# Mamba decay matrices in a two-layer kernel: a clamp and one exponential per head on ScalarE, where TensorE added a mask and ScalarE took four exponentials

## The reference

```
dA    = dt * A                                # dt > 0, A < 0: every step is negative
cum   = cumsum(dA)                            # falls along the positions of a chunk
diff  = cum[i] - cum[j]                       # per head
decay = exp(where(i >= j, diff, -inf))        # lower triangle alone, values at most 1
scores = (C_i . B_j) * decay * dt_j
Y_diag = scores @ x ;  states are carried from chunk to chunk
hidden = rmsnorm((Y + D * x) * silu(gate)) * norm_w ;  out = hidden @ out_proj_w
```

## Time and profile before

| what | value |
|---|---|
| median of three runs | 2167.99 us |
| the profiled execution | 2167.26 us, its span 2165.5 us |
| TensorE busy | 2007.6 us, 93% |
| DVE busy | 1610.2 us, 74% |
| ScalarE busy | 1274.9 us, 59% |
| POOL busy | 785.5 us, 36% |
| mean granted TensorE clock | 0.988 |
| DMA | 180.20 MB, mean 83 GB/s |
| the chain that ended last | PE 47%, issue 27%, ACT 11%, DVE 11% |
| ScalarE L1190, the four exponentials per head | 1024 instructions, 288.1 us |
| TensorE L859, the mask | 256 instructions, 77.5 us |

### The profile page before, as it was taken

One profiled execution on the slowest core, in us unless ns is written; L12 is line 12 of the kernel. 1 busy time (PEld: TensorE's weight loads), 2 busy tenths in 40 slices (PEclk: granted clock), 3 DMA queues, 4 the chain that ended last, 5 costly groups with the idle time before them and its releaser, 6 DMA issues.

```text
span 2165.5 us, 43621 instructions
## 1 busy us (share of the span) xinstructions
PE 2007.6 (93%) x12940; PEld 1652.1 (76%) x12940; DVE 1610.2 (74%) x2956; ACT 1274.9 (59%) x3110; POOL 785.5 (36%) x1128
## 2 busy tenths in 40 slices
PE   5999989999899998999989999999999999999997
PEld 4888577777688857777778885777778887677776
DVE  4774589999677458888867745888887773588886
ACT  3562388888555227777745513777774552477775
POOL 2210157777300014556530001556661000155565
PEclk9999999999999999999999999999999999999999
DMA  5330233333322002323322200232232220133321
GB/s 188 116 124 1 83 103 131 131 131 126 112 78 75 32 25 74 94 90 87 92 75 87 77 30 17 88 95 87 87 97 83 83 72 1 40 89 94 94 87 54
DMA packets 100366, 180.20 MB, mean 83 GB/s; under 512 B 8337, under 2 KB 30033, under 8 KB 100177
## 3 DMA queue, kind: packets, MB, share of 16 engines
q1 hardware_dynamic: 100304, 179.40, 26.3%
HBM read 139.52 MB, written 39.85 MB: 83 GB/s over the span
## 4 chain that ended last, share of the span: by engine, by line
PE 47%; issue 27%; ACT 11%; DVE 11%; POOL 2%; ACTq 1%; DVEq 1%; DMA 0%; POOLq 0%
PE bank L650 21%; DVE conv_acc L1337 5%; PE bank L893 4%; ACT conv_acc L1101 4%; PE bank L770 4%; ACT place L1183 4%; PE bank L868 3%; PE bank L876 3%; DVE y_in L1467 3%; PE bank L859 3%; PE bank L750 3%; PE bank L778 2%; ACT bank L1190 1%; PE bank L792 1%; DVE place L1472 1%
## 5 line engine op out<-in xcount | busy, mean ns | idle before, releaser
L650 PE MATMUL bank<-xn_r,w_r 128*128 128x512 f32 x2304 | 587.9, 404 | 18.9 <-issue 9.2
L650 PEld LDWEIGHTS bank<-xn_r,w_r 128*128 128x128 f32 x2304 | 421.9, 191 | 113.8 <-issue 24.7
L1337 DVE SCALAR_TENSOR_TENSOR conv_acc<-bank,conv_sb,conv_acc 128x511 f32<-128x511 f32 (+2 forms) x408 | 304.4, 746 | 97.9 <-ACT conv_acc L1101 80.2
L1190 ACT ACTIVATE bank<-bank,cum_neg 128x128 f32<-128x128 f32 x1024 | 288.1, 361 | 47.3 <-PE bank L859 44.2
L1031 ACT ACTIVATE place_r<-bank 128x512 fp32r<-128x512 f32 (+1 forms) x384 | 199.2, 563 | 177.7 <-PE bank L650 151.5
L1269 DVE TENSOR_TENSOR place_r<-bank,place_r 128x512 fp32r<-128x512 f32 (+1 forms) x384 | 231.0, 641 | 87.7 <-ACT place_r L1031 86.7
L650 PE MATMUL bank<-place_r 128*128 128x512 f32 (+3 forms) x1536 | 284.6, 333 | 5.3 <-DVE place_r L1269 4.5
L650 PEld LDWEIGHTS bank<-place_r 128*128 128x128 f32 x1536 | 236.9, 191 | 23.0 <-DVE place_r L1269 9.5
L543 POOL TENSOR_TENSOR carry<-state,dec 128x128 f32<-128x128 f32 x256 | 105.2, 411 | 407.1 <-ACT state L1026 385.6
L517 POOL TENSOR_TENSOR rstd<-var_eps,minus_half 128x4 f32<-128x4 f32 (+2 forms) x12 | 9.7, 807 | 665.9 <-DVE var_eps L1282 665.9
L1055 ACT ACTIVATE place<-bank,bias 128x512 f32<-128x512 f32 (+3 forms) x256 | 131.4, 526 | 161.0 <-DVE bias L1317 161.0
(11 more groups left out here) (142 smaller groups left out, 3544.6 us busy)
## 6 DMA issues: line engine op xcount, KB each, us to landing
w_r<-pair_split SPq DMA_DIRECT2D x96, 512.0 KB, 4.3
w_r<-qkv_split SPq DMA_DIRECT2D x48, 512.0 KB, 4.0
wo_r<-out_split SPq DMA_DIRECT2D x96, 256.0 KB, 2.6
pair_split<-w_r SPq DMA_DIRECT2D x32, 512.0 KB, 3.3
qkv_split<-w_r SPq DMA_DIRECT2D x16, 768.0 KB, 3.8
w_r<-qkv_split SPq DMA_DIRECT2D x48, 256.0 KB, 3.1
raw<-in_w_pair SPq DMA_DIRECT2D x32, 256.0 KB, 3.5
out_split<-wo_r SPq DMA_DIRECT2D x32, 256.0 KB, 2.0
```

The lines of the kernel that those rows point to most:

```text
L650: ins = mm(out, lhsT=w(a), rhs=m(b), start=(start and i == 0), stop=(stop and i == 2), **kw)
L1190: ins = A(bank[3 + h][:, c * P:(c + 1) * P], bank[3 + h][:, c * P:(c + 1) * P], ACT.Exp, bias=cum_neg[:, c, bass.ds(n * 2 + h, 1)])
L1337: stt(out=conv_acc[:, back:W], in0=src[:, 0:W - back], scalar=conv_sb[:, ch, TAPS - 1 - back:TAPS - back], in1=conv_acc[:, back:W], op0=AL ...
```

## The change

`causal_bf` is no longer added by TensorE: `mask_cum` and its calls go, and with them its wait for `grow`. `mixes` waits for `grow` itself (ScalarE's own `decays`). It then takes Relu(cum_j - bank) per chunk, that is max(cum_j - cum_i, 0), with the positive `cum_t` as bias and a scale of -1, in place in PSUM; it signals a semaphore of its own, waits for it, and takes one exponential exp(-value) over the head's whole bank of 512 columns. On and below the diagonal this is the same decay; above it the clamp gives exp(0) = 1, and the triangle is applied by multiplying `cb` with `upto` when DVE takes it out of PSUM, once per sequence. `causal_bf` and `ident_bf` stay for the attention stage.

```diff
@@ TensorE: mamba_start, and the loop over pairs
-                pe.wait_ge(s_cum_neg_ready, b + 1)
+                pe.wait_ge(s_cum_t_ready, b + 1)
                 pe.wait_ge(s_ffn_hid, b * FT + 7)
                 spread_cum(b, 0, 0)
                 ffn_down(b)
-                mask_cum(b, 0)
...
-            def mask_cum(b, n):
-
-                pe.wait_ge(s_grow_ev, b * NPAIR + n + 1)
-                for h, done in ((0, s_cum0_done), (1, s_cum1_done)):
-                    mm(bank[3 + h][:].rearrange("p (t i) -> p t i", t=NT), lhsT=causal_bf[:],
-                       rhs=ident_bf[:].unsqueeze(1).to_broadcast([P, NT, P]), start=False, stop=True,
-                       skip_group_check=True).then_inc(done, 1)
...
-                    if more:
-                        mask_cum(b, n + 1)
                     make_states(b, n, par)
                     in_block(b, n, par)
@@ ScalarE
                 def mixes(n, par, h):
 
-                    act.wait_ge((s_cum0_done, s_cum1_done)[h], b * NPAIR + n + 1)
+                    act.wait_ge(s_grow_ev, b * NPAIR + n + 1)
                     for c in range(NT):
-                        ins = A(bank[3 + h][:, c * P:(c + 1) * P], bank[3 + h][:, c * P:(c + 1) * P], ACT.Exp,
-                                bias=cum_neg[:, c, bass.ds(n * 2 + h, 1)])
+                        ins = A(bank[3 + h][:, c * P:(c + 1) * P], bank[3 + h][:, c * P:(c + 1) * P], ACT.Relu,
+                                bias=cum_t[:, c, bass.ds(n * 2 + h, 1)], scale=-1.0)
+                    ins.then_inc((s_span0, s_span1)[h], 1)
+                    act.wait_ge((s_span0, s_span1)[h], b * NPAIR + n + 1)
+                    ins = A(bank[3 + h][:], bank[3 + h][:], ACT.Exp, scale=-1.0)
                     ins.then_inc((s_mix_exp0, s_mix_exp1)[h], 1)
@@ DVE, once per sequence
-                dve.tensor_copy(cb[:].rearrange("p t i -> p (t i)"), bank[1][:]).then_inc(s_cb_ev, 1)
+                tt(cb[:], bank[1][:].rearrange("p (t i) -> p t i", t=NT), upto[:].unsqueeze(1).to_broadcast([P, NT, P]),
+                   ALU.mult).then_inc(s_cb_ev, 1)
                 dve.wait_ge(s_cum_turned, b + 1)
-                ts(cum_neg[:], bank[6][:].rearrange("p (t h) -> p t h", t=NT)[:, :, 0:MH], -1.0, None, ALU.mult).then_inc(s_cum_neg_ready, 1)
+                ts(cum_t[:], bank[6][:].rearrange("p (t h) -> p t h", t=NT)[:, :, 0:MH], 1.0, None, ALU.mult).then_inc(s_cum_t_ready, 1)
```

More of the change, by code:

```diff
@@ L157, in two_layers @@
         pick = sb("pick", [P, 2, 2], F32R)
-        cum_neg = sb("cum_neg", [P, NT, MH])
+        cum_t = sb("cum_t", [P, NT, MH])
         state = sb("state", [P, NT - 1, P])
@@ L228, in two_layers @@
         s_gate_ready = sem("gate_ready")
-        s_cum0_done = sem("cum0_done")
-        s_cum1_done = sem("cum1_done")
+        s_span0 = sem("span0")
+        s_span1 = sem("span1")
         s_mix_exp0 = sem("mix_exp0")
@@ L278, in two_layers @@
         s_cum_turned = sem("cum_turned")
-        s_cum_neg_ready = sem("cum_neg_ready")
+        s_cum_t_ready = sem("cum_t_ready")
         s_pick_ready = sem("pick_ready")
```

## The result

| | median us | runs us |
|---|---|---|
| before | 2168.28 | 2166.64 to 2169.62 |
| after | 2260.36 | 2259.48 to 2261.13 |

The ratio is 1.0425, 95% interval 1.0407 to 1.0443: slower by 92 us. Forecast were 2273 us and the range 2240 to 2325.

The account below looks back on a forecast made before the run. ScalarE's fixed-order list was to set the step: 8.31 + 1.26 = 9.57 us against 8.76, 72.9 us over sequences 1 to 3, plus 31.5 in sequence 0; with the end 105 us, giving 2273 us, range 2240 to 2325.

Parts of the forecast that it names:

- The two rings: Pair steps, sequences 1 to 3: the longer of ScalarE's loop (8.31 us, then 9.57) and TensorE with DVE's (8.58) sets the step.
- The mask was nearly free: TensorE's mask matmuls in each pair step: removing them shortens the loop through TensorE by 0.18 us, not 0.60, because DVE's `pair_gate` is next.
- rival B: Pair stage: ScalarE's idle time absorbs the added exponentials, DVE and TensorE set 8.58 us per step, 2146 us; chance 0.04.
- The exponential's price: ScalarE, per head: 512-column exponential 0.60 us plus 0.03 gap at its wait, 0.63 us; 1.26 per pair; bounds 0.52 to 1.02.
- The unmodified part of ScalarE's ring: ScalarE from decays through its first tap and DVE back to decays, without added work: 5.21 + 3.10 = 8.31 us.
- Edits at nothing: DVE's `cb` product, `cum_t` for `cum_neg`, and the sequence start: at most 1 us per sequence, taken as nothing.
- Who else waits: Users of later exponentials: states' copy 0.63 us later, POOL's carry 6.06 us behind decays; TensorE keeps 0.99 us of slack.
- Rival A: Pair stage: TensorE's gaps lower its clock, projections lengthen; if every third pair, 64 us more, 2337 us; chance 0.08.
- C: ScalarE: Relu and Exp in different function tables, two switches per head at 1.28 us, 657 us more, 2825 us; chance 0.01.

Follow-up runs that it names:

- half exponential: The changed kernel with each head's new exponential over 256 of the 512 columns: 2205.73 us, steps of 9.02 us in sequences 1 to 3.
- squares moved: The changed kernel with ScalarE's `squares` of pair n-2 put behind the next pair's `gate_tanh`, into the wait for DVE's `off`: 2200.68 us, steps of 8.93 us.
- waits covered: The changed kernel with the copy of the states and `hid_high` placed between each head's Relus and its exponential: 2236.21 us, steps of 9.27 to 9.28 us.

## Why the prediction was right

- *The two rings.* Right. The step is set by ScalarE's list at 9.46 us (half exponential: slope one; squares moved: the order counts, the busy time does not), and with the exponential gone by TensorE and DVE at 8.56, forecast 8.58. In sequence 0 that other ring is not one number but 8.81 and 9.39 by turns, which the prediction did not see; ScalarE's 9.84 lies above both.
- *The mask was nearly free.* Right for sequences 1 to 3: 0.20 us per step measured for the forecast 0.18. In sequence 0 rival B had about 0.2, and the run without the exponential shows nothing. In the changed kernel the mask was worth nothing anywhere.
- *The exponential's price.* Forecast 0.63 us per head. From the Relus' start to the next instruction's start is 913.09 - 911.45 = 1.64 us, against 1.02 before: 0.62. For head 1, 915.11 - 913.47 = 1.64 against 0.99: 0.65. The gap of 0.03 us was measured as 0.03; the duration is 582 and not 595 ns. The Trainium skill's rule that ScalarE reaches PSUM at lower latency (ScalarE: Activation LUTs, "Step-by-step: what each stage is for") fits in sign with 582 ns to PSUM against 595 for L1085 to SBUF, by 13 ns and not the 30 that I had tried. No run takes the same instruction to both places, and the same exponential took 638 ns with the waits covered, so what stands ahead of it counts for more here.
- *The unmodified part of ScalarE's ring* was the mis-sized term: "the pitch from one instruction into L1101 when nothing is waited for is 400.10 - 399.45 = 0.65 us". It is 916.15 - 915.63 = 0.52, and in sequence 0 (L1066 at 392.14, L1090 at 392.54) even 0.40. The row I took had no wait printed, but TensorE released that tap as well:

```profile
397.72 0.66 PE L868 MATMUL bank<-ident,place 128*128 128x128 f32 x4
...
400.10 0.78 ACT L1101 ACTIVATE conv_acc<-bank,conv_sb 128x512 f32<-128x512 f32 x1
```

The transposes started at 397.72, and the 2.40 us from there to the tap that I had used elsewhere give 400.12. So ScalarE's ring was 8.31 - 0.13 = 8.18 us in sequences 1 to 3, and with 0.62 + 0.65 it is 9.45; in sequence 0 it was 8.82 - 0.25 = 8.57 and becomes 9.84. The stages were forecast to grow by 104.4 us and grew by 85.6: of the 18.8 us between, 10.1 are in sequences 1 to 3, where this pitch makes 90 x 0.13 = 11.7, and 8.7 in sequence 0, where it makes 30 x 0.25 = 7.5.
- *Edits at nothing, and "at most 1 us" per sequence.* Not quite: 7.7 us lie outside the steps counted, two thirds of it (2.7 and 2.6 us) in the stretches behind the pair stages of sequences 2 and 3, where the granted clock is lower than before and TensorE's idle times longer. Rival A had this mechanism, but placed inside the pair stage; no run isolates it here. That 2273 was off by only 13 us is in part luck: the 7.7 us made up for part of the mis-sized pitch.
- *Who else waits.* Right in order. POOL's carry ended 915.83 - 909.79 = 6.04 us behind decays, forecast 6.06. DVE's product of head 1 waited 0.27 us for the second exponential, and DVE then still waited 1.19 us for the first tap.
- *Rivals.* A: the granted clock stayed at 1.00 in all four stages with gaps of 1.02 us in every step, so a gap of this size did not bring it down here. B: the room in ScalarE is real, but behind the one wait; it is reached only when an instruction is moved there. C: no table load stands in any pair, and the Relu ran at Exp's speed; the Trainium skill's statement that Relu is in every table set (ScalarE: Activation LUTs, "Table sets: the hidden batching unit") agrees with the trace.

## What to carry to other kernels

Where each engine's list is in fixed order, compare rings per step and not busy shares: an engine at 60% with a wait in its list can be the bound, and the slack to price against is that between its own ring and the present step (here 0.58 us, and 1.27 was added). Before replacing an operation, see what stands right behind it in time; here the removed product was worth 0.2 us per step in sequences 1 to 3 because DVE was next, and nothing in sequence 0, and swapping two TensorE calls got the same without removing anything. A row without a printed wait is no proof that nothing was waited for: check it against the known distance from the other possible releaser.

## What was not expected of the hardware

- On ScalarE four passes over 128 columns with a pointer bias took 1.12 us, one over 512 took 0.66, and one of 512 without pointer 0.58.
- A short gap in ScalarE's stream makes the instructions behind it shorter, not later or earlier: with a 0.03 us gap at the wait for the exponential, `hid_high` took 0.62 us and the tap 0.77; without the gap the same instructions took 0.69 and 0.84, at the same start pitch of 0.52. Only the last one's end reaches DVE, so 0.07 us per step was lost. The cause I did not find. In the kernel with the waits covered the Relus of a pair grow from 0.34 us for the first to 0.39 for the eighth, 0.25 us from start to start; in the changed kernel they reach 0.35 and 0.37, because the second four begin again at 0.35 behind the gap. So it builds up along a stream without gaps. It is part of why ScalarE's busy time rose by 124.6 us though the exponential alone added 149.0.
- In sequence 0 DVE's addition L1472, two SBUF inputs of 384 columns, took 0.84 and 1.35 us by turns in place of 0.55 and ended 0.41 or 0.42 us behind POOL's L566 in every pair but the first and the last, before and after the change alike (there L1465, 0.76 us).
